# In-degree count of a graph kernel: ScalarE makes step rows for four of ten chunks, and the constants of the count are made first

## The reference

```python
deg = segment_sum(jnp.ones_like(src), dst, num_segments=50000) + 1.0
dinv = jax.lax.rsqrt(deg)
norm = dinv[src] * dinv[dst]
msg = h[src] * norm[:, None]
agg = segment_sum(msg, dst, ...) + h * (dinv * dinv)[:, None]
```

## Time and profile before

| | |
|---|---|
| median of 3 runs | 1913.78 us |
| profiled execution | 1902.41 us, of it a span of 1900.7 us between first and last instruction |
| PE busy | 1566.2 us, 82% |
| DVE busy | 1328.6 us, 70% |
| ACT busy | 1230.3 us, 65% |
| POOL busy | 1018.8 us, 54% |
| mean granted clock of TensorE | 0.937 of full speed |

### The profile page before, as it was taken

One profiled execution on the slowest core, in us unless ns is written; L12 is line 12 of the kernel. 1 busy time (PEld: TensorE's weight loads), 2 busy tenths in 40 slices (PEclk: granted clock), 3 DMA queues, 4 the chain that ended last, 5 costly groups with the idle time before them and its releaser, 6 DMA issues.

```text
span 1900.7 us, 36488 instructions
## 1 busy us (share of the span) xinstructions
PE 1566.2 (82%) x8258; PEld 1092.8 (57%) x8258; DVE 1328.6 (70%) x4475; ACT 1230.3 (65%) x3127; POOL 1018.8 (54%) x1009
## 2 busy tenths in 40 slices
PE   5400499999999976988888889699999999995675
PEld 2200378887777755766766666355555555554454
DVE  7916366676666645666666665488888888886687
ACT  0285366666666633666666666477777777775899
POOL 5000466666666626666666662666666666633453
PEclk8855699999999987999999999799999999998999
DMA  8497466654444434777766665577775444428998
GB/s 262 155 342 264 152 195 193 191 180 138 136 135 138 134 131 129 259 254 255 258 200 200 196 199 180 170 227 230 229 233 157 126 131 129 127 87 289 402 333 304
DMA packets 218928, 382.41 MB, mean 201 GB/s; under 512 B 38959, under 2 KB 41228, under 8 KB 218832
## 3 DMA queue, kind: packets, MB, share of 16 engines
q1 hardware_dynamic: 190272, 342.01, 52.3%
q0 software_dynamic: 28560, 39.34, 9.3%
HBM read 222.75 MB, written 177.81 MB: 211 GB/s over the span
## 4 chain that ended last, share of the span: by engine, by line
PE 71%; DVE 7%; DMA 6%; issue 6%; ACT 6%; POOL 1%; SPq 1%; another core or an unknown queue 1%; DVEq 0%; ACTq 0%; POOLq 0%
PE bank L1337 10%; PE bank L1320 9%; PE bank L1312 9%; PE bank L1387 5%; PE bank L1304 5%; PE bank L1373 4%; PE bank L1375 4%; PE bank L1380 4%; PE bank L1379 4%; PE bank L1377 4%; ACT page L864 4%; PE bank L1356 3%; DMA page<-YT 3%; PE bank L1359 2%; PE bank L1299 2%
## 5 line engine op out<-in xcount | busy, mean ns | idle before, releaser
L668 POOL DMA_INDIRECT gath<-XP,ROWI x294 | 297.0, 1010 | 335.6 <-issue 229.0
L668 POOL DMA_INDIRECT gath<-MT,ROWI x294 | 325.0, 1105 | 206.7 <-PE bank L1387 107.0
L668 POOL DMA_INDIRECT gath<-G,ROWI x294 | 294.1, 1000 | 191.5 <-issue 93.5
L1320 PEld LDWEIGHTS bank<-w_sb,page 128*128 128x128 f32 x1568 | 191.7, 192 | 52.1 <-issue 51.8
L1337 PE MATMUL bank<-gath,onehot 128*128 128x128 f32 x1176 | 162.7, 290 | 70.3 <-issue 40.1
L752 ACT ACTIVATE page<-bank,b_sb 128x512 f32<-128x512 f32 x196 | 123.9, 683 | 113.4 <-PE bank L1312 93.3
L1320 PE MATMUL bank<-w_sb,page 128*128 128x128 f32 x1568 | 192.8, 276 | 5.1 <-issue 5.1
L1337 PEld LDWEIGHTS bank<-gath,onehot 128*128 128x128 f32 x1176 | 144.6, 198 | 78.3 <-issue 62.8
L1312 PE MATMUL bank<-page,w_sb 128*128 128x512 f32 x392 | 185.1, 595 | 0.0
L1063 DVE TENSOR_TENSOR page<-bank,DINV 128x512 f32<-128x512 f32 x98 | 67.8, 691 | 159.2 <-PE bank L1320 134.2
L1092 DVE TENSOR_TENSOR page<-bank,page 128x512 f32<-128x512 f32 x98 | 67.8, 692 | 146.5 <-PE bank L1337 125.0
(11 more groups left out here) (213 smaller groups left out, 3574.2 us busy)
## 6 DMA issues: line engine op xcount, KB each, us to landing
page<-YT SPq DMA_DIRECT2D x196, 256.0 KB, 4.5
MT<-page SPq DMA_DIRECT2D x98, 260.0 KB
XP<-page SPq DMA_DIRECT2D x98, 256.0 KB, 2.2
G<-page SPq DMA_DIRECT2D x98, 256.0 KB
OWN<-page SPq DMA_DIRECT2D x98, 256.0 KB
page<-OWN SPq DMA_DIRECT2D x98, 256.0 KB
YT<-page SPq DMA_DIRECT2D x98, 256.0 KB
page<-AD SPq DMA_DIRECT2D x98, 256.0 KB
```

Of the source, the lines that this page charges most:

```text
L668: nc.gpsimd.indirect_dma_start(gath[k][:, w, 0:width], None, rows, bass.IndirectOffsetOnAxis(ap=ROWI[:, at:at + 1], axis=0), bounds_check= ...
L1320: last = nc.tensor.matmul(bank[6 + k][:, j * D:(j + 1) * D], rows[k][:, j * P:(j + 1) * P], w2_sb[:, h, :], start=(h == 0), stop=(h == 1))
```

## The change

The batch grows from 8 to 10 chunks (`PAIRS` = 5), which gives 19 batches and a rest of 3 pairs. In a full batch DVE makes `oh_lo` for all 5 pairs, but `oh_hi` only for the first 3. For the other two pairs (`STEPPED` = 2, four chunks) ACT makes step rows: Sign(c - hi + 0.5) over the 393 columns c = -1 to 391, that is -1 for every column below the edge's tile and +1 from it on, by one ACTIVATE of 393 columns with a bias from `hi_s` for each chunk. PE adds up `oh_lo` times steps in bank 2. The difference of neighbouring columns is then twice the number of edges in a tile, so that deg = (difference + 2) / 2 + the counts of bank 0; the one instruction after the count becomes three. In the rest all 3 pairs are made by DVE.

POOL makes `col_h` and the new `col_s` ahead of the other constants, and DVE's first batch waits for `col_h` alone. DVE's steps change their order: the split into `hi` and `lo` and the new `hi_s` first, then `one_hots(0)`, then `last_f` and `ended`, `one_hots(1)`, `coarse_i`, `one_hots(2)` and `one_hots(3)`, then the wait for `c_row` and what hangs on it, then the other batches.

```diff
-PAIRS = 4
+PAIRS = 5
+STEPPED = 2
...
+        col_s = early("col_s", [P, NT + 1], F16)
+        hi_s = early("hi_s", [P, ET])
...
-        oh_hi = early("oh_hi", [P, OH_SLOTS, PAIRS, NT, 2], BF16)
+        oh_hi = early("oh_hi", [P, OH_SLOTS, PAIRS - STEPPED, NT, 2], BF16)
+        step_hi = early("step_hi", [P, OH_SLOTS, 2 * STEPPED, NT + 2], BF16)
...
-        win_eq = after_hi[:, 5 * W * P:5 * W * P + (W + 1) * P].rearrange("p (w e) -> p w e", w=W + 1)
+        after_steps = step_hi[:].rearrange("p s n c -> p (s n c)").bitcast(F32)
+        win_eq = after_steps[:, 0:(W + 1) * P].rearrange("p (w e) -> p w e", w=W + 1)
...
-        CONSTS = 14
+        CONSTS = 15
...
+            nc.gpsimd.iota(col_h[:], [[1, NT], [0, 2]], base=0, channel_multiplier=0, **exact).then_inc(consts, 1)
+            nc.gpsimd.iota(col_s[:], [[1, NT + 1]], base=-1, channel_multiplier=0, **exact).then_inc(consts, 1)
             nc.gpsimd.iota(bound_c[:, 0:1], [[0, 1]], base=FAST_COLS[0][0], channel_multiplier=GN, **exact).then_inc(consts, 1)
...
-            nc.gpsimd.iota(col_h[:], [[1, NT], [0, 2]], base=0, channel_multiplier=0, **exact).then_inc(consts, 1)
...
-            pool.wait_ge(consts, 12)
+            pool.wait_ge(consts, 13)
...
         def _(act):
+            act.wait_ge(consts, 2)
+            act.wait_ge(oh_ready, 1)
+            for n in range(BATCHES):
+                slot = n % OH_SLOTS
+                wait(act, oh_used, n + 1 - OH_SLOTS)
+                for c in range(2 * STEPPED):
+                    at = 2 * (n * PAIRS + PAIRS - STEPPED) + c
+                    last = nc.scalar.activation(step_hi[:, slot, c, 0:NT + 1], col_s[:], ACT.Sign, bias=hi_s[:, at:at + 1])
+                last.then_inc(steps_ready, 1)
             act.wait_ge(w_loaded, 16 * W_LOADS)
             act.wait_ge(deg_plus, 1)
...
             dve.wait_ge(loaded, 32)
-            link(nc.vector.tensor_copy(last_f[:], dst_e[:, ET - 1:ET]))
-            dve.wait_ge(consts, 6)
-            nc.vector.tensor_scalar(ended[:], bound_r[:], last_f[:, 0:1], None, ALU.is_gt).then_inc(coarse, 1)
             nc.vector.tensor_scalar(hi_i[:], dst_e[:], 7, None, ALU.logical_shift_right)
             link(nc.vector.tensor_scalar(lo_i[:], dst_e[:], P - 1, None, ALU.bitwise_and))
+            nc.vector.tensor_scalar(hi_s[:], hi_i[:], -1.0, 0.5, ALU.mult, ALU.add).then_inc(oh_ready, 1)
...
-            dve.wait_ge(consts, CONSTS)
+            dve.wait_ge(consts, 1)
...
-                one_hot_pairs(oh_lo, lo_f, P)
-                one_hot_pairs(oh_hi, hi_f, NT).then_inc(oh_ready, 1)
+                one_hot_pairs(oh_lo, lo_f, P, pairs)
+                one_hot_pairs(oh_hi, hi_f, NT, tested).then_inc(oh_ready, 1)

             one_hots(0)
+            link(nc.vector.tensor_copy(last_f[:], dst_e[:, ET - 1:ET]))
+            dve.wait_ge(consts, CONSTS)
+            nc.vector.tensor_scalar(ended[:], bound_r[:], last_f[:, 0:1], None, ALU.is_gt).then_inc(coarse, 1)
+            one_hots(1)
             q = slice(0, NG)
             dve.wait_ge(coarse, 2)
...
-            one_hots(1)
             one_hots(2)
+            one_hots(3)
             dve.wait_ge(c_rows, 16 * W)
...
-            for n in range(3, BATCHES + 1):
+            for n in range(4, BATCHES + 1):
                 one_hots(n)
             dve.wait_ge(oh_used, BATCHES + 1)
-            nc.vector.tensor_scalar(deg[:], bank[0][:, 0:NT], 1.0, None, ALU.add).then_inc(deg_plus, 1)
+            link(nc.vector.tensor_copy(t_b[:], bank[2][:, 0:NT]))
+            link(nc.vector.scalar_tensor_tensor(t_a[:], bank[2][:, 1:NT + 1], 2.0, t_b[:], ALU.add, ALU.subtract))
+            nc.vector.scalar_tensor_tensor(deg[:], t_a[:], 0.5, bank[0][:, 0:NT], ALU.mult, ALU.add).then_inc(deg_plus, 1)
...
-                pe.wait_ge(oh_ready, n + 1)
-                for b in range(pairs):
+                pairs, tested = (PAIRS, PAIRS - STEPPED) if n < BATCHES else (REST, REST)
+                pe.wait_ge(oh_ready, n + 2)
+                for b in range(tested):
...
+                if tested < pairs:
+                    pe.wait_ge(steps_ready, n + 1)
+                for b in range(tested, pairs):
+                    for c in range(2):
+                        last = nc.tensor.matmul(bank[2][:, 0:NT + 1], oh_lo[:, slot, b, :, c], step_hi[:, slot, 2 * (b - tested) + c, 0:NT + 1],
...
                 last.then_inc(oh_used, 1)
```

More of the change, by code:

```diff
@@ L357, in build_gnn @@
         oh_used = sem("oh_used")
+        steps_ready = sem("steps_ready")
         deg_plus = sem("deg_plus")
@@ L884, in _, with one_hot_pairs @@
             dve.wait_ge(loaded, 32)
-            link(nc.vector.tensor_copy(last_f[:], dst_e[:, ET - 1:ET]))
-            dve.wait_ge(consts, 6)
-            nc.vector.tensor_scalar(ended[:], bound_r[:], last_f[:, 0:1], None, ALU.is_gt).then_inc(coarse, 1)
             nc.vector.tensor_scalar(hi_i[:], dst_e[:], 7, None, ALU.logical_shift_right)
             link(nc.vector.tensor_scalar(lo_i[:], dst_e[:], P - 1, None, ALU.bitwise_and))
+            nc.vector.tensor_scalar(hi_s[:], hi_i[:], -1.0, 0.5, ALU.mult, ALU.add).then_inc(oh_ready, 1)
             nc.vector.tensor_copy(hi_f.rearrange("p n b -> p (n b)"), hi_i[:])
             link(nc.vector.tensor_copy(lo_f.rearrange("p n b -> p (n b)"), lo_i[:]))
-            dve.wait_ge(consts, CONSTS)
+            dve.wait_ge(consts, 1)
             def one_hots(n):
-                slot, at, pairs = n % OH_SLOTS, n * PAIRS, PAIRS if n < BATCHES else REST
+                slot, at = n % OH_SLOTS, n * PAIRS
+                pairs, tested = (PAIRS, PAIRS - STEPPED) if n < BATCHES else (REST, REST)
                 wait(dve, oh_used, n + 1 - OH_SLOTS)
-                def one_hot_pairs(made, parts, width):
+                def one_hot_pairs(made, parts, width, pairs):
                     return nc.vector.tensor_tensor(made[:, slot, 0:pairs], col_h[:, 0:width, :].unsqueeze(1).to_broadcast([P, pairs, width, 2]),
                                                    parts[:, at:at + pairs, :].unsqueeze(2).to_broadcast([P, pairs, width, 2]), ALU.is_equal)
-                one_hot_pairs(oh_lo, lo_f, P)
-                one_hot_pairs(oh_hi, hi_f, NT).then_inc(oh_ready, 1)
+                one_hot_pairs(oh_lo, lo_f, P, pairs)
+                one_hot_pairs(oh_hi, hi_f, NT, tested).then_inc(oh_ready, 1)
             one_hots(0)
+            link(nc.vector.tensor_copy(last_f[:], dst_e[:, ET - 1:ET]))
+            dve.wait_ge(consts, CONSTS)
+            nc.vector.tensor_scalar(ended[:], bound_r[:], last_f[:, 0:1], None, ALU.is_gt).then_inc(coarse, 1)
+            one_hots(1)
             q = slice(0, NG)
@@ L1252, in _ @@
             for n in range(BATCHES + 1):
-                slot, pairs = n % OH_SLOTS, PAIRS if n < BATCHES else REST
-                pe.wait_ge(oh_ready, n + 1)
-                for b in range(pairs):
+                slot = n % OH_SLOTS
+                pairs, tested = (PAIRS, PAIRS - STEPPED) if n < BATCHES else (REST, REST)
+                pe.wait_ge(oh_ready, n + 2)
+                for b in range(tested):
                     for c in range(2):
@@ L1258, in _ @@
                                                 start=n == 0 and b + c == 0, stop=n == BATCHES and b == pairs - 1 and c == 1,
+                                                skip_group_check=True)
+                if tested < pairs:
[3 more added lines that the diff above has]
+                        last = nc.tensor.matmul(bank[2][:, 0:NT + 1], oh_lo[:, slot, b, :, c], step_hi[:, slot, 2 * (b - tested) + c, 0:NT + 1],
+                                                start=n == 0 and b == tested and c == 0, stop=n == BATCHES - 1 and b == pairs - 1 and c == 1,
                                                 skip_group_check=True)
```

## The result

The changed kernel takes 1893.68 us (median of 4 runs, 1890.42 to 1896.62); the kernel before 1914.6 beside it (4 runs, 1913.1 to 1918.57). The ratio is 0.9894, with a 95% interval of 0.988 to 0.9907, so 20.9 us less, between 17.8 and 23. I had said 12.6 less, 1901.2, with a range down to 1897.0. The direction was right, the size was not.

What follows compares the result with a forecast made beforehand. VectorE's count, in its loop with PE, was taken to bound the time before DINV. Start, `c_row` wait, slow stretch and 2.09 us batches put the table load at 63.6, not 76.19: 1913.78 - 12.6 = 1901.2 us, range 1897.0 to 1906.5.

Steps and rivals of the forecast that it cites:

- its loop with PE: In the count's batches: with two slots, DVE's batch n + 2 waits for PE's n; 4.18 us for two, 2.09 each.
- the cover of ScalarE: In each batch: four Signs take 2.06 us, just under the 2.09 loop, so ACT stays hidden, thinly.
- `col_s` at 0.52: At the start, on POOL: making `col_s` was taken as 0.5 us, with 2.2 as the dear case.
- the five integer steps behind `col_h`: At the start: DVE's steps stand until `col_h` ends at 5.3, then take 1.68 us; first batch at 7.0.
- The wait for `c_row`: Early in the count: `coarse_i` at 12.0 plus 11.07 us puts `c_rowf` at 23.1; DVE idles 4.0, batch 4 at 25.05.
- the rival: `c_row` comes late, POOL's issues slowed by busier DVE: three at 5.15 us leave a gain of 3.5, 1910.3; chance 0.09.
- The second slow stretch: Behind `c_row`'s wait: PE stands, its clock falls, and batch 8 begins at 35.5 instead of 33.4; 2.1 us.
- the 2.1 of the clock: In the forecast's own range of 10 to 15 us gained: 2.1 us more if TensorE's clock holds.
- dear end of 2.47: ACT's upper end for four Signs in a batch, no overlap: 2.47 us, against 2.06 taken.
- the rival of the clock: TensorE stays at its lower clock through the count: table load at about 77.4, +1.2 us, 1915.0; chance 0.04.
- ScalarE as the bound: In the count: ACT needs 2.47 us a batch, 4.2 more over batches 8 to 18; gain 8.4, 1905.4; chance 0.08.
- one table load: At the count's end: Sign's table set also holds the square root, so the 1.28 us load goes; 1899.9; chance 0.12.

Runs made afterwards that it cites:

- the pause: Seven reciprocals (18.4 us) added on VectorE between last batch and degree: kernel before ratio 1.0104; changed kernel 1.0011 and 0.9999, all against the kernel before.
- e10: Changed kernel with `coarse_i` ahead of `one_hots(1)` instead of behind it: 1889.18 us, ratio 0.9895 to the kernel before.
- e3: Kernel before with the new order alone, 8 chunks to a batch, all on VectorE: 1825.18 us, ratio 0.9978 to the kernel before.
- e4: Changed kernel with the old order, so only ScalarE's steps and batches of 10 chunks: 1814.03 us, ratio 0.9916 to the kernel before.
- e1: Changed kernel once more, no edits, with its own trace: 1813.92 us, ratio 0.9912 to the kernel before.
- e14: Changed kernel with `c_row`'s wait behind `one_hots(5)`, its countings between batches, and an early Sqrt: 1886.74 us, ratio 0.9881 to the kernel before.

## Why the prediction was wrong

**Right:** that VectorE's work and its loop with PE bound the count, that the gain at DINV passes on through the scaling (from DINV to POOL's first gather it is 122.0 to 125.5 us in all traces of either kernel, with the pause and without), the new period (2.05 against 2.09), the prices of all new instructions, the cover of ScalarE and of its first table load, `col_s` at 0.52, the five integer steps behind `col_h` (the first took 1.68 us from 3.73 and ended at 5.41), the table load that stays. The Trainium skill's figures for ScalarE ("ScalarE: Activation LUTs", section "What ACT_TABLE_LOAD costs") gave an estimate of 0.514 for a Sign in a row; 52 of them in 26.82 us are 0.516.

**The step that failed is "The wait for `c_row`".** I carried the 11.07 us from `coarse_i` to `c_rowf` over whole. They contain three POOL issues of 3.03, 2.32 and 0.96 us, and I had read them: in the rival I said that they grow beside VectorE, and let them only grow. My own schedule had VectorE stand from 12.0 to 14.3, just where the first issues now fall; by the 0.96 in the same rows they had to shrink. They took 1.19, 0.97 and 0.97, 3.2 us less in all. That it is VectorE's batch beside the first issue that makes the difference is shown by e10, where that batch alone was moved, and e3 and e4 agree. Mis-sized: 11.07 for 8.20 (8.05 to 8.84 in the six traces).

**"The second slow stretch"** was mis-sized beside it in the first trace: 2.1 for 1.3 (9.50 for batches 4 to 7 less 4 x 2.05). It doesn't follow from the late `c_row`, since e1 with 4.55 us of standing and e4 with 7.65 pay 1.3 as well. Two of six traces pay 2.4, so 2.1 was no bad guess for one execution; what was wrong was to expect the same stretch each time. Before, too, has two lengths of it, 10.2 us in two traces and 6.8 in three. e14 shows what all of such standing costs together with the wait and the load: 4.0 against the first trace.

**The range** was the third mistake. Its lower end, 16.8 us gained, is about the forecast with the 2.1 of the clock and the 1.28 of the table load (16.0), and no case had `c_row` earlier. `c_row` had a price for coming later and none for coming earlier, so the range was no bound on that side.

**Slips in the sums** that change little: four Signs at 0.51 are 2.04 and not 2.06, the dear end of 2.47 comes out as 2.44 (four at 0.61 without overlap), and in the rival of the clock 75.0 and three instructions of 0.60 give 76.8 and not 77.4.

**What the runs don't settle** is the rest of the result. DINV moved by 15.6 to 17.2 us in four traces of after against four of before; the timed gains are 20.9, 16.1 and 17.6 on three chips (intervals 17.8 to 23, 13 to 19.2, 13.9 to 20.1). The lower end of the first interval is 0.6 above the largest of the shifts. The pauses show no sign that a microsecond ahead of DINV counts for more than one, and the traces show no gain behind it. That the first comparison's 20.9 is partly its four runs of before is a reading, not shown: what lies behind DINV varies by 5 to 6 us between executions. So of the 8.3 us between forecast and result 4.5 are found in the count, and 3.8 stay open.

The rivals: neither a late `c_row`, nor ScalarE as the bound, nor TensorE at its lower level came about, and one table load didn't serve both functions (a second one stands at 59.08).

## To carry to other kernels

Where work is reordered, don't carry over a latency whole: take it apart into what is fixed and what depended on the neighbour, and look at who is the neighbour now; it can get shorter too. A transfer that GpSimd issues belongs where VectorE stands anyway, and short work that makes TensorE stand can go between batches, one piece at a time. Before a small difference is read from two traces, ask of each stretch whether it is the same in a second trace of the same kernel: here one stretch of the count cost 1.3 or 2.4 us with the same program.

## What the hardware showed

- An indirect DMA's issue on POOL took 0.96 to 1.2 us with VectorE idle. The first issue beside a batch of two-operand `tensor_tensor` in 16 bits took 2.75 to 3.03 and ended 1.05 us after that batch. Later issues that were held up ended 0.84 to 0.85 us after an instruction of VectorE: the third of e1 at 17.10 (16.26), the second of before at 16.69 (15.84), and one of 4.61 us in after at 27.02 (26.18), behind two whole batches.
- Not every issue beside a batch is held up: the third one took 0.97 in after, where it began just before the batch's second instruction (14.95 and 14.97), and 2.16 in e1, where it began just behind it (14.94 and 14.88).
- The granted clock fell to its lower level behind a standing of 2.11 us in one kernel and stayed up behind the same 2.11 us in another. With the same program the stretch at the lower level was 3.4 us long in four traces and 6.8 in two.
- The table load on the path cost what its row says, and no more: with it moved ahead, VectorE waited 0.66 us for the root instead of 1.93, so 1.27 were saved. The Trainium skill ("ScalarE: Activation LUTs", section "What ACT_TABLE_LOAD costs") adds 1.38 us of draining to each switch of tables; neither the saving nor the rows have room for it, since the load begins at 59.08 and the root at 60.37.
- The same program takes 1830 us in two of the groups and 1908 to 1915 in three; the norm pass alone is 421 us in the one and 488 in the other, with 243 GB/s moved in the faster and 210 in the slower.
